# A graph convolution kernel with its first 160 edge tiles turned into a matrix of 256 nodes by all nodes

## The reference

```
f  = layernorm(x)
agg(z)[n] = sum over edges e with dst[e] == n of edge_weight[e] * z[src[e]]
h  = agg(f @ W1) + b1
z  = leaky(concat(h, f[root]))            # root: one row for all nodes
c  = leaky(agg(z @ W2) + b2)              # second convolution
x1 = x + leaky(concat(c, h[root]) @ Wl + bl)
g  = layernorm(x1); score = g @ wr + br
out = x1 + g + (gelu(g @ w1 + b1) @ w2 * score, for the 3124 rows of highest score, else 0)
```

## Time and profile before

| | us |
|---|---|
| median of 3 runs | 2071.18 (2070.89 to 2073.11) |
| profiled execution: its span, and own time | 2915.3 |
| first convolution's gathers from f begin | 89.5 |
| last gather issued, first convolution | 1414.8 |
| first gather issued, second convolution | 1445.3 |
| last gather issued, second convolution | 2808.6 |
| last add of a group into acc | 2844.0 |
| end | 2915.3 |

### The profile page before, as it was taken

How to read it: one execution, slowest core, us unless ns; L and a number is a source line. 1 busy time by engine, 2 the same in 40 slices (tenths; PEclk the granted TensorE clock), 3 DMA queues, 4 the chain that set the end, 5 groups by cost and what they waited for, 6 DMA issues and landing times.

```text
span 2915.3 us, 49425 instructions
## 1 busy us (share of the span) xinstructions
PE 1865.9 (64%) x7011; PEld 1437.8 (49%) x7012; DVE 1169.0 (40%) x4136; ACT 369.1 (13%) x927; POOL 1474.9 (51%) x1571
## 2 busy tenths in 40 slices
PE   0465646655555556354637888886777686757687
PEld 0344535434443444333526666665666465645475
DVE  6543333332332332222324455444544434434356
ACT  4200000000000000000101111111111111111111
POOL 5455555554555554455344555555555554545430
PEclk9788778777776776767878889988988888978797
DMA  6422222222222322222432222222222222222212
GB/s 202 131 83 81 80 80 80 84 78 74 82 81 78 88 79 75 70 79 77 152 98 72 72 72 81 78 79 75 78 81 76 81 71 69 83 62 82 67 50 88
DMA packets 120873, 244.27 MB, mean 84 GB/s; under 512 B 32822, under 2 KB 71046, under 8 KB 120748
## 3 DMA queue, kind: packets, MB, share of 16 engines
q0 software_dynamic: 73664, 200.90, 24.0%
q1 hardware_dynamic: 35612, 32.02, 3.5%
q10 hardware_dynamic: 11472, 10.27, 1.1%
HBM read 223.42 MB, written 19.64 MB: 83 GB/s over the span
## 4 chain that ended last, share of the span: by engine, by line
SPq 53%; issue 35%; PE 5%; DVE 3%; DVEq 1%; another core or an unknown queue 1%; DMA 1%; ACT 1%; ACTq 0%
SPq L348 45%; SPq L343 7%; PE ps_agg L716 2%; PE ps_dn L854 1%; PE ps_up L865 1%; DVE fw2s L1062 1%; DVE S L1153 0%; ACT xs L480 0%; DVE ring L1442 0%; DMA normed_rows<-xs 0%; DVEq L1193 0%; PE ps_o L804 0%; DVE acc L1161 0%; PE ps_dn L852 0%
## 5 line engine op out<-in xcount | busy, mean ns | idle before, releaser
L716 PE MATMUL ps_agg<-ring,S 128*128 x3136 | 912.1, 440 | 677.0 <-SPq L355 320.3
L716 PEld LDWEIGHTS ps_agg<-ring,S 128*128 128x128 f32 x3136 | 669.1, 221 | 860.1 <-issue 757.8
L434 POOL DMA_INDIRECT ring<-conv_rows,idx x752 | 714.5, 950 | 632.4 <-DVEq L1188 424.2
L434 POOL DMA_INDIRECT ring<-normed_rows,idx x736 | 701.1, 953 | 631.7 <-DVEq L1188 426.7
L1153 DVE TENSOR_SCALAR S<-iota,dstc,wc 128x128 f32<-128x128 int16 x1584 | 454.9, 353 | 377.1 <-issue 360.3
L1161 DVE TENSOR_TENSOR acc<-acc,ps_agg x490 | 206.3, 421 | 893.4 <-PE ps_agg L716 478.4
L716 PE MATMUL ps_agg<-ring,S_more 128*128 x768 | 265.7, 506 | 254.6 <-DVE S_more L1153 150.0
L716 PEld LDWEIGHTS ps_agg<-ring,S_more 128*128 128x128 f32 x768 | 187.6, 254 | 321.3 <-issue 287.9
L854 PE MATMUL ps_dn<-fw2s,hT 128*128 128x256 f32 x848 | 232.7, 434 | 0.0
L854 PEld LDWEIGHTS ps_dn<-fw2s,hT 128*128 128x128 f32 x848 | 179.4, 218 | 49.5 <-issue 21.7
L865 PE MATMUL ps_up<-xnT,fw1s 128*128 128x256 f32 x800 | 195.0, 400 | 8.9 <-issue 7.1
(11 more groups left out here) (248 smaller groups left out, 1077.2 us busy)
## 6 DMA issues: line engine op xcount, KB each, us to landing
ring<-normed_rows SPq DMA_DIRECT2D x2048, 1.0 KB
ring<-conv_rows SPq DMA_DIRECT2D x2048, 1.0 KB
ring<-conv_rows,idx POOLq DMA_INDIRECT x752
ring<-normed_rows,idx POOLq DMA_INDIRECT x736
conv_rows<-rows ACTq DMA_DIRECT2D x49, 128.0 KB
xs<-in_x SPq DMA_DIRECT2D x6, 640.0 KB
out_rows<-xs SPq DMA_DIRECT2D x3, 1024.0 KB
xs<-in_x SPq DMA_DIRECT2D x2, 1280.0 KB
```

The lines of the kernel that those rows point to most:

```text
L434: pool.indirect_dma_start(out=ring[:, slot * TG + t, :], out_offset=None, in_=rows_of, in_offset=bass.IndirectOffsetOnAxis(ap=at, axis=0)) ...
L716: last = nc.tensor.matmul(to, select[:, t, :], moving, start=(t == 0), stop=(t == TG - 1))
```

## The change

Sixty-four empty edges are put in front of the edge list, so that the tiles shift by half a tile. The first 160 of the 784 tiles (NM) are no longer gathered. All of their edges point to nodes 0 to 255 and are put into one matrix A of 256 rows (destinations) by 6,272 columns (sources): entry (d, s) is the sum of the weights of the edges from s to d. The remaining 624 tiles are gathered by POOL alone, in rounds of three groups (QG = 3), so there are 52 rounds; 622 gathers a convolution, the first 22 of the first convolution from x. The ring holds 6 groups.

**Building.** Rounds 1 to 40 of the first convolution each build four of these tiles. DVE makes two one-hot matrices a tile, behind the first group (hot_tiles): one of the source's low 7 bits (128 wide) and one of (destination offset, source window), 5 x 49 = 245 wide, times the weight. PE multiplies them behind the second group (build_tiles), and DVE adds the 128 x 49 x 5 product into A, which lies in xs, behind the third group (add_tiles), at a place that it loads into a register for each tile. ACT clears xs for this beforehand. A tile whose edges span more than 5 destinations would set off a slow path; with this input the largest span is 4.

**Use.** In rounds 41 to 50 of the first convolution DVE copies 5 of A's column blocks (copy_chunk), PE multiplies them with the rows of f that SP has loaded (dense_chunk, 10 matmuls), and DVE adds 512 columns (add_chunk). SP stores A to DRAM in five pieces. In the second convolution each round starts with two matmuls of one block of A and one of the new rows (dense_block), both loaded by SP, and one more add 512 wide (add_block) behind the first group's add. Then SP loads x again into xs.

**Moved.** In a group DVE now adds first (add_last), then releases the ring and builds the selection matrices ahead. Three pieces a round instead of four: conv_step and ffn_step_b stand together behind the third group. The steps begin in round 6, so that 46 lie in the rounds and 2 of each convolution follow behind them. Two wide comparisons for near_rows (line 1297) move behind the rounds of the first convolution.

```diff
-    QG = 4
+    QG = 3
...
+    LEAD = P // 2
+    CR = -(-(E + LEAD) // (CH * P))
...
+    NIT = NW + 3
...
-    FAR_EVERY, FAR_Q = 3, 1
-    FARS = (NIT - 1) // FAR_EVERY
...
+    NM = NT - NIT * RING
...
+    SPAN = 5
+    KEYS = SPAN * NW
+    BPER = 4
+    B_IT = 1 + NM // BPER
...
+    PIECES = 5
+    RAWG = 6
...
+            def load_chunk(j):
+                a0 = NW - (j + 1) * CHUNK
+                skip = max(0, -a0)
+                slot = (j & 1) * CHUNK
+                sp.dma_start(blocks[:, slot + skip:slot + CHUNK, :], f_dram[(a0 + skip) * P:(a0 + CHUNK) * P, :].rearrange("(w p) d -> p w d", p=P)).then_inc(chunk_loaded[j & 1], 16)
+            for j in range(2):
+                load_chunk(j)
+            sp.wait_ge(build_added, NM + BPER + 1)
...
+            for i in range(PIECES):
+                w0, w1 = i * NX // PIECES, (i + 1) * NX // PIECES
+                sp.dma_start(a_dram[:, w0:w1, :], xs[:, w0:w1, :]).then_inc(matrix_stored, 16)
+            for j in range(2, CHUNKS):
+                sp.wait_ge(dense_done, B_IT + j - 1)
+                load_chunk(j)
...
+            def load_block(i):
+                a = max(0, NW - 1 - i)
+                m = a + 1 if i < NW else 0
+                sp.dma_start(block_a, a_dram[:, m, :]).then_inc(block_loaded, 16)
+                sp.wait_ge(t2_stored, 16 * (NW - a + 2))
+                sp.dma_start(block_t, t2_dram[a * P:(a + 1) * P, :]).then_inc(block_loaded, 16)
...
-            def far_tile(l, rows_of, n, b, before):
-                k = within(sp.snap(n * -1 + (FARS - 1)), FARS - 1)
-                if before is not None:
-                    sp.wait_ge(group_used[l], n * (FAR_EVERY * QG) + 1)
-                for c in range(P // FAR_PASS):
-                    _, offsets = nc.values_load_multi_w_load_instructions(
-                        bass.at_runtime_partition(far[0:1, c * FAR_PASS:(c + 1) * FAR_PASS], k), engines=(mybir.EngineType.SP,),
-                        min_val=0, max_val=(N - 1) * D * 4, skip_runtime_bounds_check_because="the table holds clamped values")
-                    for i in range(FAR_PASS):
-                        p = c * FAR_PASS + i
-                        sp.dma_start(ring[p:p + 1, SLOTS * TG + b, :].bitcast(i8), rows_of[ds(offsets[i], D * 4)].unsqueeze(0)).then_inc(far_landed[l][b], 16)
-                    if c == 0 and before is not None:
-                        far_done(l, 1 - b, before)
...
+            for i in range(1, NIT):
+                sp.wait_ge(block_used, i)
+                load_block(i)
...
-                    by_sp = q == FAR_Q and it > 0 and it % FAR_EVERY == 0
-                    for t in range(TG - 1 if by_sp else TG):
-                        tile = (NIT - 1 - it) * RING + q * TG + t
+                        pool.wait_ge(group_used[l], g - SLOTS + 2)
...
-                        at = idx_far[:, q * TG + t:q * TG + t + 1] if early else idx[:, tile:tile + 1]
+                        at = idx_near[:, q * TG + t:q * TG + t + 1] if early else idx[:, tile:tile + 1]
                         pool.indirect_dma_start(out=ring[:, slot * TG + t, :], out_offset=None, in_=rows_of,
-                                                in_offset=bass.IndirectOffsetOnAxis(ap=at, axis=0)).then_inc(landed[slot // QG][q], 32 if by_sp and t == 0 else 16)
+                                                in_offset=bass.IndirectOffsetOnAxis(ap=at, axis=0)).then_inc(landed[slot // QG][q], 16)
...
+            for c in STORES:
...
+                nc.scalar.activation(xs[:, w0:w1, :], zeros[:, 0:1].unsqueeze(2).to_broadcast([P, w1 - w0, D]), ACT.Copy).then_inc(matrix_cleared, 1)
...
+            def build_tiles(it):
+                pe.wait_ge(build_added, it * BPER + 1)
+                pe.wait_ge(build_ready, it)
+                for t in range(BPER):
+                    last = nc.tensor.matmul(up_banks[:, t // 2, t % 2 * KEYS:(t % 2 + 1) * KEYS], src_hot[:, t, :], key_hot[:, t, :], start=True, stop=True)
+                last.then_inc(build_done, 1)
...
+            def dense_chunk(it):
+                half = within(pe.snap((it + B_IT) & 1), 1)
+                to = up_banks[:, ds(half, 1), :].rearrange("p b n -> p (b n)")
...
+                for m in range(MW):
+                    for k in range(CHUNK):
+                        row = within(pe.snap(f0 + k), 2 * CHUNK - 1) if k else f0
+                        last = nc.tensor.matmul(to[:, m * D:(m + 1) * D], chunk_a[:, k, m * P:(m + 1) * P], flat(blocks[:, ds(row, 1), :]), start=(k == 0), stop=(k == CHUNK - 1))
+                last.then_inc(dense_done, 1)
...
+            def dense_block(it):
+                e0 = within(pe.snap(extras), NG * NW)
+                i = within(pe.snap(e0 + it * PER[1]), MOST)
+                pe.wait_ge(block_loaded, it * 32 + 32)
+                pe.wait_ge(acc_step[1], i + 1)
+                for m in range(MW):
+                    to = flat(ps_agg[:, ds(i & 1, 1), m * D:(m + 1) * D])
+                    last = nc.tensor.matmul(to, block_a[:, m * P:(m + 1) * P], block_t, start=True, stop=True)
+                last.then_inc(mm_done[1], 1)
...
+            def edge_round(l, it, steps, s=None, matrix_work=True):
+                if l == 1:
+                    dense_block(it)
+                for q in range(QG):
+                    edge_group(l, it, q)
+                    if l == 0 and q == 1 and matrix_work:
+                        first_nodes(it)
+                    for piece in steps[q] if steps else ():
+                        piece(s)
...
+            rounds(0, ((), (turn_step0,), (h_step0,)), NW - 1, first_root_term)
...
+            rounds(1, ((turn_step1,), (ffn_step_a,), (conv_step1, ffn_step_b)), NW - 1, late_weights_in)
...
+            def add_block(i):
+                dve.wait_ge(mm_done[1], i + 1)
+                dve.wait_ge(acc_step[1], i + 1)
+                dve.sem_inc(block_used, 1)
+                V.tensor_tensor(first_acc, first_acc, flat(ps_agg[:, ds((i + 1) & 1, 1), :]), op=ALU.add).then_inc(acc_step[1], 1)
...
+            def hot_tiles(it):
+                for t in range(BPER):
+                    at = within(dve.snap(it * BPER + (t - BPER)), NM - 1)
+                    V.tensor_scalar(src_hot[:, t, :], iota[:, 0:P], src_low[:, ds(at, 1)], None, ALU.is_equal)
+                    last = V.tensor_scalar(key_hot[:, t, :], iota[:, 0:KEYS], keys[:, ds(at, 1)], wc[:, ds(at, 1)], ALU.is_equal, ALU.mult)
+                last.then_inc(build_ready, 1)
+            def add_tiles(it):
+                dve.wait_ge(matrix_cleared, len(XCH))
+                for t in range(BPER):
+                    at = within(dve.snap(it * BPER + (t - BPER)), NM - 1)
+                    base = within(dve.value_load(base_row[0:1, ds(at, 1)]), MSPAN - SPAN)
+                    to = matrix[:, :, ds(base, SPAN)]
+                    if t == 0:
+                        dve.wait_ge(build_done, it)
+                    dve.wait_ge(build_added, it * BPER + (t + 1))
+                    of = up_banks[:, t // 2, t % 2 * KEYS:(t % 2 + 1) * KEYS].rearrange("p (r a) -> p a r", a=NW)
+                    V.tensor_tensor(to, to, of, op=ALU.add).then_inc(build_added, 1)
+            def copy_chunk(it):
+                a0 = within(dve.snap(it * -CHUNK + (NW + 1 - CHUNK + B_IT * CHUNK)), NW + 1 - CHUNK)
+                dve.wait_ge(build_added, NM + BPER + 1)
+                V.tensor_copy(chunk_a, xs[:, ds(a0, CHUNK), :]).then_inc(chunk_copied, 1)
+            def add_chunk(it, done):
+                of = up_banks[:, ds(within(dve.snap((it + B_IT) & 1), 1), 1), :].rearrange("p b n -> p (b n)")
+                dve.wait_ge(dense_done, it + 1)
+                dve.wait_ge(acc_step[0], done)
+                V.tensor_tensor(first_acc, first_acc, of, op=ALU.add).then_inc(dense_added, 1)
...
                 for q in range(QG):
-                    select_ahead(l, it, q)
...
                     e0 = within(dve.snap(extras), NG * NW)
                     e1 = within(dve.snap(e0 + more), NG * NW)
-                    p0 = within(dve.snap(e0 + it * QG + q), NG * (NW + 1))
-                    add_last(l, p0)
+                    p0 = within(dve.snap(e0 + it * PER[l] + (q + l)), MOST)
+                    if l == 1 and q == 0:
+                        add_last(l, p0 - 1)
+                    else:
+                        if q == 0:
+                            dve.wait_ge(dense_added, it + 2)
+                        add_last(l, p0)
                     dve.sem_inc(group_used[l], 1)
+                    select_ahead(l, it, q)
...
+            rounds(0, (z_step0, no_step, zero_step0), NW - 1, lambda: z_step0(NW - 1), first_root_row)
+            near_rows()
...
+            rounds(1, (x1_step, norm_step, no_step), NW - 1, last_norm, lambda: dve.wait_ge(x_again, 16 * (len(XCH) + len(PART))))
```

More of the change, by code:

```diff
@@ L513, in rounds @@
                 with act.Fori(0, stop) as s:
-                    for q in range(QG):
-                        steps[q](s)
```

(47 more changed lines are left out.)

368 lines of the change are left out of this document (217 added, 151 removed).

## The result

| | us, median | ratio to before, 95% interval |
|---|---|---|
| before | 2071.03 | |
| changed | 2131.68 (2127.11 to 2136.26) | 1.0295 [1.0275, 1.0315] |
| changed, a second time beside other kernels | 2128.90 | 1.0255 [1.0228, 1.0283] |

The change makes the kernel 2.9% slower. The forecast was 2022, and the time lies outside its range of 1905 to 2125. The slower side had a chance of 0.32, but with another mechanism than the one that struck.

The account below looks back on a forecast made before the run. POOL was taken to bound both convolutions before the change, DVE after it. 1021 + 8 + 92 + 810 + 24 + 71 = 2026 us, less 4 by which the sum for before exceeded the runs, gave 2022; range 1905 to 2125.

Parts of the forecast that it names:

- POOL bounds the kernel before: Both convolutions before the change: gathers start 1.25 us apart, 19.5 us a round, and SP's row gathers are hidden.
- Its ledger: Sum for the kernel before from POOL's gathers, gaps and end: 2075 us, set against the median of 2071.18.
- The first convolution: After the change DVE bounds it, 18.1 us a build round and 15.5 in rounds 41 to 50; over at 1021.
- This pace is the recording's: SP's 183 row gathers at 0.66 us each, 85 us a tile, were put down to profiling, not the timed runs.
- the 112 us: First convolution: most that 320 new DVE comparisons could delay POOL through the shared port, 2.8 us a round.
- Rival (B): Build rounds of the first convolution: DVE-PE hand-overs and colder PE make them 20.6 us or more, 2122 total; chance 0.32.
- PE stands 1 us under DVE: Second convolution after the change: PE needs 16.5 us a round, against DVE's 17.6.
- 46 x 17.6 = 810: Second convolution: 46 rounds with steps at DVE's 17.6 us each, 810 us.
- PE's round: Second convolution after the change: 3.9 sums at 1.73, the window's steps at 8.9 and 0.9 make 16.5 us.
- Rival (C): Second convolution: PE or PE-DVE turns bound it, 18.5 us a round, 41 us more, 2063; inside the forecast's chance of 0.54.
- The extra: DVE's price for a group's extra sum: 3.0 us each, 2.65 us a round in both convolutions.
- The two steps behind the rounds: End of the second convolution: two steps that lie behind the rounds, at 12 us each, 24 us.

Follow-up runs that it names:

- POOL-gathers-all: Kernel before, with the tiles that SP fetched row by row gathered by POOL like all others, no matrix: 2121.04 us, ratio 1.0229 on a chip without stalls.
- piece-first runs of before: Kernel before, with PE's piece of each group issued ahead of the group's extra sum, nothing else changed: 2074.43 us, ratio to before 1.0001.
- PE's piece first: Changed kernel, with PE's piece of each group issued behind the group's sum and ahead of its extra sum: 2017.16 us, ratio to before 0.9726.

## Why the prediction was wrong, step by step

**POOL bounds the kernel before: right**, and shown by the POOL-gathers-all and the piece-first runs of before. Its ledger hit 2075 with two errors that cancelled, which was luck. The first convolution hands over at 1007.5, not 1038: POOL resumes at 94.0 instead of 120.0, which had been read from a chip with stalls, and the step to the second convolution's first gather is 1.7 us instead of 13, against 7 us of waits that the ledger left out. The second needs 1064, not 1037, since POOL waits some 28 us in it. "This pace is the recording's" was wrong in its cause, and right in the part that mattered, that SP is hidden in the 2071 us.

**The first convolution: better than forecast.** 926.7 to the second's first gather, not 1021. 28 us of it are the start; build rounds took 16.7 instead of 18.0 (40 of them, 53 us), the chunk rounds 14.7 instead of 15.5, the end the rest. hot_tiles took 2.3 us (of 2.9 with its branch) and add_tiles 2.4 (0.65 a tile instead of 0.82). The gathers kept their pace beside the new comparisons: 0.96 us on the mean for those that lay beside DVE's comparisons and for those that did not, so nothing of the 112 us that the prediction allowed for at most showed. Here the change gained some 81 us against before (1007.5). Rival (B) had the right side and the wrong place: build rounds lay 2.6 us under its point of decision (19.3).

**The step that failed: "PE stands 1 us under DVE", and with it "46 x 17.6 = 810".** Rounds 6 to 51 of the second convolution took 998.7 us from their first release to their last, about 1001 with the last group's end, 21.8 each, 191 more than the sum had. Two terms were mis-sized.
- *PE's round.* The steps were put at 8.9 us from a count of matmuls at 1.73/8 (42 of them are 9.1); they take 10.8 in the trace (16.9 less 0.87 for the block and 3 x 1.73), of which 1.6 are PE's idle time at turn and gelu, a term that the prediction left at nothing. By its own figures PE's round without an extra was 3 x 1.73 + 8.9 + 0.9 = 15.0, no less than DVE's; it is 16.9. That is some 90 us over 46 rounds. Rival (C) named PE as the bound, at 18.5 a round, with chance inside the forecast's, and priced it at 41 us; it was the case that came, at over four times that.
- *The extra.* 3.0 us was DVE's price, and the same at each group. The price of a turn is what the other engine can't do in it, so it depends on the place: behind the second group PE's next piece is long, and stands behind the extra in its order. Against a clean round of 16.9 it cost 7.9 us there, 17 times, 84 us over the 3.0. The other 20 extras of these rounds cost 87 us together, 27 over the 3.0 each. Against that the 37 extras are 11 us less at 3.0 than the 2.65 a round of the sum. 90 + 84 + 27 - 11 is 190.

The sum with the measured terms: 926.7 + 24.8 to the first release + 79.4 for rounds 0 to 5 + 998.7 to the last release + 98.7 to the end = 2128.3. The two steps behind the rounds were about right: 98.7 us from the last release to the end, in both traces of the changed kernel, 77.8 before, 21 for two steps against 24.

**Against before** the second convolution, from its first gather to the end, takes 1201 us where it took 1064: POOL had 49 rounds of 19.5 in which all turns hid; its pace is 15.0 now, and nothing took its place but the turns. The 180 us that the matrix saves POOL there were not to be had while PE needs 16.9 us a round and more for each extra. With PE's piece first the second convolution takes 1101 and the whole 2017, 2.7% under before and by chance near the forecast's 2022.

## What to carry to other kernels

When a change takes the bounding engine away, read the next bound as the order in which two engines hand over, not as the busier one's sum: write down for each wait what the waiting engine has next in its order, and put its long independent piece ahead of the wait, not behind it. Price a conditional part at every place where it can fall, since here the same extra cost 4 to 5 us at two places and 8 at the third. And before any of it, compare a profile's span with the timed runs; where they differ by 40%, take rows of another run before building on its start and end.

## What the hardware showed that was not expected

The same kernel before took 2071 to 2074 us on some chips and 2910 to 2949 on others, in timed runs too. On the latter a register instruction with a median of 69 ns takes up to 1386. This shows on DVE, PE and SP, not on ACT (69 at most), while gathers, comparisons and adds keep their durations: POOL is busy for 1209.2 us there in the changed kernel and for 1209.9 on the other kind. PE, which waits more, has a mean clock of 0.871 instead of 0.923. A change of 2.9% for the worse is there one of 16% for the better (0.8380). About half of that, 8%, comes from SP's 4096 single-row DMAs with their register moves, as the kernel shows in which POOL gathers all. What gives the rest was not taken apart; in that kernel's trace POOL waits 564 us for DVE's release.
